# The first group's load and normalisation ahead of the weights' preparation, and a weight product that waits for its own two loads

## What is computed

```python
kn  = kv / jnp.maximum(jnp.linalg.norm(kv, axis=-1, keepdims=True), EPS_NORM)
kp  = kn @ Wi.T + bi
hdd = jax.nn.silu(kp @ Wl1.T + bl1)
hdd = jax.nn.silu(hdd @ Wl2.T + bl2)
```

## Time and profile before

| | us |
|---|---|
| median of three runs | 1922.48 |
| the profiled execution | 1923.33 |
| its span, first to last instruction | 1921.6 |
| TensorE busy (matmul) | 1790.6 (93%) |
| VectorE busy | 1497.3 (78%) |
| ScalarE busy | 1070.8 (56%) |
| GpSimd busy | 624.1 (32%) |
| TensorE's first matmul starts | 10.59 |
| H1(0) starts | 24.08 |

### The profile page before, as it was taken

The page is one execution under the profiler, slowest core; times in us unless marked ns, Lnnn a source line. Parts: engine busy times, 40 slices in busy tenths (PEclk is TensorE's granted clock), DMA queues, the critical chain, the costliest instruction groups (busy, mean ns, idle before and its releaser), DMA issues.

```text
span 1921.6 us, 30942 instructions
## 1 busy us (share of the span) xinstructions
PE 1790.6 (93%) x11218; PEld 1585.2 (82%) x11218; DVE 1497.3 (78%) x3900; ACT 1070.8 (56%) x1733; POOL 624.1 (32%) x927
## 2 busy tenths in 40 slices
PE   6999999999999999999659995989999499999996
PEld 4878788888888888888659995878988499999996
DVE  5777579899999999999748884789998466666663
ACT  4566734556666666666456662565564255555552
POOL 3112001223443333344614443134534312222333
PEclk9999999999999999999779997999999599999998
DMA  4446231223222222211143422134322212222210
GB/s 151 158 141 200 78 134 65 85 83 111 97 85 82 82 70 81 67 40 38 41 140 129 144 88 88 56 117 138 99 88 76 89 59 81 92 81 80 76 54 20
DMA packets 132607, 176.90 MB, mean 92 GB/s; under 512 B 11486, under 2 KB 115813, under 8 KB 132328
## 3 DMA queue, kind: packets, MB, share of 16 engines
q1 hardware_dynamic: 121704, 159.87, 25.9%
q0 software_dynamic: 10752, 15.06, 2.3%
HBM read 113.25 MB, written 76.51 MB: 99 GB/s over the span
## 4 chain that ended last, share of the span: by engine, by line
PE 86%; DVE 5%; issue 3%; ACT 2%; POOL 2%; DMA 2%; SPq 0%; POOLq 0%; DVEq 0%; ACTq 0%
PE ps L385 77%; PE ps L409 4%; PE ps L701 2%; PE ps L690 1%; POOL d_p L2540 1%; DVE bst L1568 1%; PE ps L462 1%; DMA stage<-in_w 0%; DMA wl_t<-in_Wl2T 0%; DVE rO L2108 0%; DMA d_x<-df 0%; DVE pay L1892 0%; SPq L2735 0%; DMA d_p<-pay,sut 0%; DVE wslotA L1773 0%
## 5 line engine op out<-in xcount | busy, mean ns | idle before, releaser
L385 PE MATMUL ps<-wslotA,fh 128*128 128x256 f32 x1776 | 326.1, 284 | 0.0
L1783 DVE TENSOR_TENSOR fl<-fF,fh 128x512 fp32r<-128x512 f32 x316 | 214.1, 683 | 95.6 <-ACT fF L1163 94.0
L385 PEld LDWEIGHTS ps<-wslotA,fh 128*128 128x128 f32 x1776 | 280.4, 191 | 5.2 <-DVE fl L1783 0.2
L385 PE MATMUL ps<-wslotA,fl 128*128 128x256 f32 x888 | 251.2, 283 | 0.0
L2535 POOL TENSOR_TENSOR smalls<-smalls,powers 128x4 f32<-128x4 f32 x87 | 27.9, 321 | 594.1 <-DVE smalls L1571 593.9
L2540 POOL DMA_INDIRECT d_p<-pay,sut x128 | 154.0, 1203 | 105.5 <-DVE pay L1940 58.3
L385 PE MATMUL ps<-x2h,wslotA 128*128 128x512 f32 x512 | 171.0, 396 | 0.2 <-DVE x2l L1593 0.2
L385 PEld LDWEIGHTS ps<-wslotA,fl 128*128 128x128 f32 x888 | 170.0, 191 | 0.0
L1162 ACT ACTIVATE fh<-ps,b1e 128x512 fp32r<-128x512 f32 x126 | 86.9, 690 | 144.6 <-PE ps L385 127.6
L385 PE MATMUL ps<-wslotB,fh 128*128 128x256 f32 x752 | 137.1, 283 | 0.0
L385 PE MATMUL ps<-eh,wslotB 128*128 128x512 f32 x384 | 127.4, 398 | 4.5 <-DVE el L1964 4.5
(11 more groups left out here) (374 smaller groups left out, 5053.5 us busy)
## 6 DMA issues: line engine op xcount, KB each, us to landing
stage<-in_w SPq DMA_DIRECT2D x16, 1024.0 KB
d_p<-blank SPq DMA_DIRECT2D x24, 528.0 KB, 4.7
pay<-d_p SPq DMA_DIRECT2D x24, 528.0 KB
d_x<-df SPq DMA_DIRECT2D x16, 516.0 KB, 3.4
xA<-d_x SPq DMA_DIRECT2D x16, 516.0 KB
xa<-in_x SPq DMA_DIRECT2D x16, 512.0 KB, 4.8
d_h<-hh SPq DMA_DIRECT2D x16, 512.0 KB, 5.6
d_h<-hl SPq DMA_DIRECT2D x16, 512.0 KB, 2.7
```

The costliest lines, as they stand in the source:

```text
L385: return pe.matmul(o, a, b, start=start, stop=stop, skip_group_check=True)
L1783: ve.tensor_tensor(dl[:, half(k)], df_[:, half(k)], f32(dh[:, half(k)]), ALU.subtract).then_inc(S["low"], 1)
```

## The change

SP issues first_x(0) ahead of the loads of Wi and Wl1T instead of behind them. Wl2T raises a semaphore of its own, prep_wl2; TensorE's prepare() waits for prep_pe = 32 (Wi and Wl1T), and ScalarE's copy of Wl2 for prep_wl2 = 16. On VectorE prepare_weights() stands behind stats1(1) and norm1(0) instead of ahead of them. The semaphore cvec is gone: the memset that raised it raises prep_dve, and the three waits for prep_dve by prepare_weights() go from 1 to 2.

```diff
@@ TensorE prepare, h2
-                pe.wait_ge(S["prep_pe"], 48)
+                pe.wait_ge(S["prep_pe"], 32)
                 ps = unit("W1P")
                 mm256(ps, wi_v, wl1_v).then_inc(S["mpe"], 1)
...
-                    pe.wait_ge(S["prep_dve"], 1)
+                    pe.wait_ge(S["prep_dve"], 2)
@@ ScalarE prepare
-                act.wait_ge(S["prep_pe"], 48)
+                act.wait_ge(S["prep_wl2"], 16)
                 copy(wl2_h, wl2_v).then_inc(S["prep_act"], 1)
@@ VectorE prepare, router_weights
-                ve.memset(blank[:, 260:261].bitcast(U), 1000000).then_inc(S["cvec"], 1)
+                ve.memset(blank[:, 260:261].bitcast(U), 1000000).then_inc(S["prep_dve"], 1)
...
-                    ve.wait_ge(S["prep_dve"], 1)
+                    ve.wait_ge(S["prep_dve"], 2)
@@ VectorE order
             prepare()
             stats1(0)
-            prepare_weights()
             stats1(1)
             norm1(0)
+            prepare_weights()
             lows(kl, kh, ring.of("T1", 0), S["kh"], 0)
@@ SP fill, load_xl
-                    sp.wait_ge(S["cvec"], 1)
+                    sp.wait_ge(S["prep_dve"], 1)
...
-                    sp.wait_ge(S["prep_dve"], 1)
+                    sp.wait_ge(S["prep_dve"], 2)
@@ SP order
+            first_x(0)
             square(wi_v, "Wi", S["prep_pe"])
             square(wl1_v, "Wl1T", S["prep_pe"])
-            first_x(0)
             load(cols[:, 0:22], io["cols_c"], S["cols"])
             load(cols[:, 22:23], io["fgate"].partition_broadcast(128), S["cols"])
             load(cols[:, 23:24], io["lrate"].partition_broadcast(128), S["cols"])
             first_x(1)
-            square(wl2_v, "Wl2T", S["prep_pe"])
+            square(wl2_v, "Wl2T", S["prep_wl2"])
             first_x(2)
```

More of the change, by code:

```diff
@@ L104, in build @@
         S = {n: sem(n) for n in (
-            "consts", "cvec", "dve", "pool", "cols", "late", "fill", "stage", "stage_b", "whi", "wl",
-            "prep_pe", "prep_act", "prep_dve", "var_a", "rst_a", "kn", "knT", "kh", "h1", "si1", "fl", "h2", "hf",
+            "consts", "dve", "pool", "cols", "late", "fill", "stage", "stage_b", "whi", "wl",
+            "prep_pe", "prep_wl2", "prep_act", "prep_dve", "var_a", "rst_a", "kn", "knT", "kh", "h1", "si1", "fl", "h2", "hf",
             "htok", "ka", "kb", "rh", "hl", "gram", "nm", "slP", "slpe", "slact", "slpool", "sldve",
```

## The result

The changed kernel takes 1915.69 us in the median (1913.41 to 1917.21, 7 runs), the kernel before, run beside it, 1921.76 us (1919.25 to 1924.41, 7 runs). The ratio, taken over all these runs, is 0.9966 with an interval of 0.9954 to 0.9977, about 6.5 us; the medians differ by 6.1. The profiled execution took 1916.66 us, with a span of 1914.9 against 1921.6, 6.7 us less. Every engine's busy time is that of before within 1 us: nothing was removed but waiting.

A forecast was written before the change was run, and what follows sets the result against it. The prediction took the kernel as TensorE-bound, its first 40 us held by a chain through Wl2T, the product and VectorE's weight preparation. H1(0) 6.9 us sooner (24.08 - 17.18) gave 1922.48 - 6.9 = 1915.6 us, range 1912.7 to 1918.8.

The forecast's parts named there:

- x(1) at 9.7: First loads: x(1) lands at 9.7 us, bounds 9.2 and 10.45, and becomes the first link of the chain.
- The product off the chain, with 1.8 us of cover: TensorE's weight product starts about 6.6 and ends at 11.9, 1.8 us before VectorE takes its results up at 13.75.
- kn(0) at 13.75: VectorE: after stats1(1) (1.9 us) and norm1(0) (2.1 us), kn(0) is there at 13.75, not 20.65.
- prepare_weights for nothing, with a margin of 0.2: VectorE: its 1.62 us run from 13.75 to 15.37 beside T1(0), costing nothing if done by 15.57.
- H1(0) at 17.18, H2(0) near 24.7: TensorE: H1(0) starts at 17.18 instead of 24.08, 6.9 us sooner, and H2(0) starts near 24.7.
- Nothing given back: Behind H1(0): the program moves as a block, so the 6.9 us saved in the head stays whole.
- Rival A: Head: TensorE's clock is up for T1(0) and H1(0), H2(0) 8.4 to 8.5 us sooner, 1914.1 us; chance 0.25.
- Rival B: First loads: x(1) lands late; at 16.3 leaves 0.3 us of gain, 1922.2 us; chance 0.05.
- C: Blocks behind H1(0): TensorE's clock rises later, 2.35 us more per block; five blocks give 1927.3 us; chance 0.03.
- D: Changes of phase (945:1000, 1490:1550): lower clock held longer gives back up to 3 us, 1918.6 us; chance 0.07.

The follow-up runs named there:

- e7: Changed kernel with the load of x(1) right behind x(0), ahead of Wi and Wl1T; ratio to the kernel before 0.9959.
- e1: Kernel before with only VectorE's new order, SP's order and the product's wait for all three weights kept; ratio 0.9976, 4.6 us.
- e6: Changed kernel with the load of x(1) issued ahead of the three small loads into cols; ratio to the kernel before 0.9955.
- e8: Changed kernel with norm1(0) and prepare_weights() right behind stats1(0), and stats1(1) behind the low parts of kh; ratio to the kernel before 0.9951.
- e5: Changed kernel with unused filler matmuls on TensorE, 20 ahead of the wait for Wi and Wl1T, 16 behind the product; ratio to the kernel before 0.9953.
- e10: e7 with filler matmuls ahead of the product (16), behind it (3) and behind T1(0) (5); 1913.20 us, ratio to the kernel before 0.9943.
- e9: e8 with filler matmuls ahead of the product (12), behind it (5) and behind T1(0) (5); ratio to the kernel before 0.9959.
- e11: The repetition: the changed kernel measured once more, unaltered, beside e9 and e10; ratio to the kernel before 0.9953, 9 us.
- e4: Changed kernel with the load of x(1) issued last of the first batch; ratio to the kernel before 1.0005.

## Why the prediction was right

The forecast was 1915.6, the measured median 1915.69. Agreement to 0.1 us is luck: the kernel before measured 1921.76 beside it and not 1922.48, so the saving was 6.1 to 6.7 us where 6.9 was forecast, and the repetition gave 9. The mechanism is what was right, and each step can be held against a row.

- *x(1) at 9.7:* 9.81 in the profile. In the other executions with this place in SP's order it landed between 8.6 and 10.2, a wider spread than the bounds of 9.2 and 10.45 that I gave from one trace; it is the largest uncertainty of the sum.
- *The product off the chain, with 1.8 us of cover:* it ran from 6.56 to 11.82, and TensorE then idled 2.17. With x(1) put ahead of it (e7) the product started 1.6 us later, which alone would not have used up the 2.17, and kn(0) was ready 2.3 sooner (11.65 against 13.92); together they put the product on the chain by 1.7 us (13.39 against 11.65).
- *kn(0) at 13.75:* 12.54 + 1.38 = 13.92, the 0.1 of x(1) and 0.07.
- *prepare_weights for nothing, with a margin of 0.2:* right, and the margin was larger, 0.57. The 1.62 us that I took from before held a wait for TensorE between L1606 and L1610; without it the three take 1.34.
- *H1(0) at 17.18, H2(0) near 24.7:* 17.36 and 24.92.
- *Nothing given back:* right, within the 2 us or so by which the span behind H2(0) differs anyway.
- *Rival A* (the clock up for T1(0) and H1(0)) did not occur in the profiled execution, and its half did in others: for T1(0) and not for H1(0), in e1, e6, e8 and the repetition. Where it was forced (e5) it gave 1.3 us for H1(0), near the 1.2 of the working, and H2(0) lost it again. Only e10 kept it through both. It should have been weighed as something that differs from execution to execution, worth 0.7 us where T1(0) alone is fast, and not as one case for all.
- *Rival B* (x(1) late) was right in its mechanism and shown on purpose; its price was too low, since I took the fall of the DMA engines' busy share, near 16.3, for the landing of the last load, which came at 18.0, so that the gain ends on the other side of nothing.
- *Rivals C and D* did not occur in the changed kernel: its clock rose 5 us into H1(0), as before, H2(0) took 3.04 us against 3.05, and the stretches at the changes of phase held what they held within about 1 us. A milder form of C, H2(0) at the lower level for a part, came in e5, e8 and e9.
- *The Trainium skill's* warning ("DMA: Bandwidth & Descriptors", section "Queues, rings and completion order", on landings out of order) did not come true here: in the changed kernel x(0), Wi, Wl1T and x(1) landed at 5.0, 5.7, 6.4 and 9.8, in the order of issue. What the Trainium skill says of the clock ("TensorE: Matmul & The Clock Gate", section "What's actually happening", activity releases the throttle) agrees with the filler run, where the first part of the product took 1.89 us behind 7.4 us of fillers and 3.75 without.

## What to carry to other kernels

Two edits can remove much of the same wait: alone, each gave about 4.5 us, together 6.5 and not 9, so a part that is tried by itself tells little of the sum. Put work that only needs its own operands in front of work that waits for another engine, and let a product wait for what it reads; then look up which load is the new first link, and how much cover the displaced work has left. A saving in the head of a long kernel can come through whole when every later wait is for an event of the kernel itself. The span behind a common point, compared before and after, is the quickest test of it, if the point lies behind the place where the clock has settled (here H2(1)) and several executions tell how far that span varies by itself (here by up to 2 us).

## What had not been expected of the hardware

- The same load in the same place of the queue took 4.8 to 6.4 us to land in different executions (x(1), 512 KB, issued at 3.79), which alone moves this kernel by 1.6 us.
- TensorE's clock rose in the product in one execution of the changed kernel and not in the other (the bias part 1.09 us in e11 against 1.71), and fell again at about 13.8, just before T1(0) ended at 13.87 (TensorE had idled 1.63 us ahead of it), so that H1(0) started at the lower level.
- The granted clock column shows only a part of this. In the changed kernel's first profile it reads 1.00 through the head although all up to H1(0) ran at the lower level. In e11 it reads 1.00 during the product too, and then 0.50 from 14 to 20, when H1(0) ran at the lower level. So it missed the level that the program started at and showed the later fall; the durations of records of one shape tell the level in both.
- Shortening one busy stretch can cost the clock of the next: H1(0) at the upper level left 3.35 us idle ahead of T1(1) in e9, and H2(0) ran at the lower level nearly to its end. It did so in part in e8 (2.03 us idle ahead of T1(1)) and in e5 (0.89 ahead of T1(1), 1.26 ahead of H2(0)), but not in e10 (0.88 and 1.25), so the length of the pause alone does not tell.
- The fall of the DMA engines' busy share is not yet the landing of the last load: in e4 the share was down to 0.10 in 16:18, and x(1) landed near 18.0.
